# Fourteen unused products at the start of a vision-transformer kernel, while its embedding weights land

## The reference

```python
h = tok(x)                       # layernorm(768) -> @ W + bias -> layernorm(256) -> + positions, class tokens
h = h + attn0(layernorm(h))      # 16 heads, causal; weights quantised by the mean of |w|
h = h + tanh(layernorm(h) @ weight @ aux1 @ aux2 + bias)
h = h + attn1(layernorm(h))      # 16 heads, biases, head mask
h = h + moe(layernorm(h))        # top 1 of 16 experts, 256 -> 1024 -> 256, capacity 76
```

## Time and profile before

| | |
|---|---|
| median of 3 runs | 361.79 us (361.61 to 362.27) |
| profiled execution | 363.0 us |
| its span | 361.2 us |
| TensorE busy | 332.7 us (92% of the span) |
| VectorE, ScalarE, GpSimd busy | 193.6, 173.9, 170.2 us |
| mean granted clock of TensorE | 0.966 |

### The profile page before, as it was taken

How to read it: one execution, slowest core, us unless ns; L and a number is a source line. 1 busy time by engine, 2 the same in 40 slices (tenths; PEclk the granted TensorE clock), 3 DMA queues, 4 the chain that set the end, 5 groups by cost and what they waited for, 6 DMA issues and landing times.

```text
span 361.2 us, 8897 instructions
## 1 busy us (share of the span) xinstructions
PE 332.7 (92%) x3230; PEld 241.1 (67%) x3230; DVE 193.6 (54%) x520; ACT 173.9 (48%) x505; POOL 170.2 (47%) x289
## 2 busy tenths in 40 slices
PE   1975998999999999999999998979899999999993
PEld 1854887787888887878788876759356455454361
DVE  0376364576857648577686888681153252351350
ACT  1680685544566566666756655360253143342350
POOL 0255289765666757676977666643002102112012
PEclk9996799999999999999999999687999999999999
DMA  7999910114361724155523222412999999993500
GB/s 237 410 355 390 368 32 28 52 52 141 102 211 58 250 78 151 54 165 178 184 76 113 83 78 77 154 38 80 392 370 409 361 365 367 312 373 104 163 12 10
DMA packets 40835, 67.11 MB, mean 186 GB/s; under 512 B 4942, under 2 KB 31889, under 8 KB 39961
## 3 DMA queue, kind: packets, MB, share of 16 engines
q1 hardware_dynamic: 36696, 57.29, 45.8%
q10 hardware_dynamic: 2448, 7.03, 5.3%
q0 software_dynamic: 1648, 2.24, 1.8%
HBM read 54.14 MB, written 8.48 MB: 173 GB/s over the span
## 4 chain that ended last, share of the span: by engine, by line
PE 76%; DMA 7%; POOL 6%; SPq 3%; DVE 3%; issue 3%; ACT 0%; POOLq 0%; DVEq 0%
PE bank L1057 12%; PE bank L1024 12%; PE bank L921 8%; PE bank L969 7%; PE bank L950 5%; PE bank L983 5%; PE bank L932 5%; PE bank L958 5%; PE bank L1035 3%; PE bank L990 3%; DMA early<-in_ffn 3%; SPq L675 3%; DMA mid<-in_table 3%; PE bank L897 2%; PE bank L906 2%
## 5 line engine op out<-in xcount | busy, mean ns | idle before, releaser
L832 POOL DMA_INDIRECT out<-mid,idx x12 | 11.7, 976 | 97.6 <-DVE mid L1412 97.6
L791 POOL TENSOR_TENSOR mid<-mid,tab 128x608 f32<-128x608 f32 x32 | 39.3, 1235 | 15.2 <-PE bank L950 11.9
L1057 PE MATMUL bank<-early,mid 128*64 128x256 f32 (+1 forms) x448 | 43.7, 381 | 0.0
L1209 ACT ACTIVATE mid<-bank,cols 128x64 f32<-128x64 f32 (+1 forms) x128 | 25.8, 332 | 25.1 <-PE bank L1035 25.1
L1322 DVE TENSOR_REDUCE mx<-bank 102x16 f32<-102x608 f32 x32 | 25.0, 783 | 22.8 <-PE bank L950 22.6
L1024 PE MATMUL bank<-early,mid 128*64 128x512 f32 (+1 forms) x192 | 36.2, 596 | 0.7 <-ACT mid L1192 0.7
L1057 PEld LDWEIGHTS bank<-early,mid 128*64 128x64 f32 (+1 forms) x448 | 25.2, 123 | 15.8 <-issue 2.9
L921 PE MATMUL bank<-xnT,attn 128*128 128x256 f32 (+1 forms) x160 | 34.9, 371 | 0.0
L897 PE MATMUL bank<-early 128*128 128x256 f32 (+2 forms) x120 | 30.0, 406 | 2.8 <-DVE tokens L1301 2.8
L921 PEld LDWEIGHTS bank<-xnT,attn 128*128 128x128 f32 x160 | 29.1, 190 | 3.6 <-issue 0.4
L776 POOL TENSOR_TENSOR rs<-rs,mhalf 128x1 f32<-128x1 f32 (+2 forms) x50 | 28.7, 574 | 4.2
(11 more groups left out here) (142 smaller groups left out, 649.3 us busy)
## 6 DMA issues: line engine op xcount, KB each, us to landing
early<-in_w SPq DMA_DIRECT2D x52, 512.0 KB, 7.1
v3a<-vt SPq DMA_DIRECT2D x102, 40.0 KB
early<-vt SPq DMA_DIRECT2D x90, 40.0 KB
expert_in<-k_empty SPq DMA_DIRECT2D x1, 3084.0 KB, 22.4
early<-in_xt ACTq DMA_DIRECT2D x2, 1152.0 KB, 19.7
early<-in_xf SPq DMA_DIRECT2D x2, 1152.0 KB, 11.7
xnT<-in_w SPq DMA_DIRECT2D x4, 512.0 KB
tokens<-in_w SPq DMA_DIRECT2D x4, 512.0 KB
```

Source lines behind the costliest of these rows:

```text
L791: eng.tensor_tensor(km[:, n % 2], bc(kT[:, :, n * PCOLS:(n + 1) * PCOLS], 2, 4), bc(bc(quarterm[:, :], 2, PCOLS), 1, KC), ALU.mult).then_i ...
L1057: ins = mm(Yp[m % 2][a * width:(a + 1) * width, 0:DIM], hT[:, m % 2, c, a * width:(a + 1) * width], w2s[e % W2_SLOTS][:, c, :], start=c == ...
L1209: ins = eng.activation(hT[:, m % 2, c, a * width:(a + 1) * width], Tp[0][:, c * 128 + a * width:c * 128 + (a + 1) * width], ACT.Relu, bias ...
```

## The change

Ahead of TensorE's list of steps it now waits for `ones` and runs fourteen products of `ones` with itself, 128x128 by 128x128 in float32, into the two halves of `Sp` in turn. Nobody reads them. The lists of all engines stay as they are.

```diff
                     pe.wait_ge(g_free[b], m)
                 return G[b], g_full[b]
 
+            pe.wait_ge(consts, 1)
+            for n in range(14):
+                mm(Sp[:, n % 2, 0:128], ones[:, :], ones[:, :], start=True, stop=True)
             done = {}
             for kind, l, n in order("pe"):
                 done[kind] = done.get(kind, 0) + 1
```

## The result

The changed kernel takes 364.26 us (median of 14 runs, 362.98 to 367.52), the kernel before 362.22 us in the same series (14 runs, 359.77 to 366.63). The ratio is 1.0064 with a 95% interval of 1.0034 to 1.0094, which is 2.3 us. The forecast was 362.1 us and no measurable change; 0.4 us of the distance to it is the kernel before itself, which stood at 361.79 us when the forecast was made. The profiled execution took 363.97 us, its span is 362.2 us.

The account below looks back on a forecast made before the run. The start was taken as bound by the landing of `in_ffn`, which fB waits for. Products 0, faster cs 0 at the end, fetch +0.3 us on 361.79 gave 362.1 us, range 360.9 to 363.0.

Parts of the forecast that it names:

- part 1: TensorE's start: the fourteen products, 28 records from about 1.15 us, take 3.1 to 5.9 us, ending before the weights at 7.84.
- part 2: First product cs: with the clock raised, its start to that of bs takes 2.6 us instead of 5.01, gaining 2.4 us.
- Its condition: Ahead of cs: the raised clock stays up over 1 to 2 us of idling; otherwise the gain at cs is 0.
- part 3: From cs to fB: of 2.4 us won, 1.5 remain after qs and become wait for `in_ffn`; gain at the end 0.
- part 4: TensorE's code on q8: 56 more instructions move its first packet ahead of the landing of `in_ffn`, delaying fB by 0.3 us.
- bounds of 0 and 1.1 us: Delay of fB: 0 if the fetching engine is early or the fetch doesn't move, 1.1 us if the whole packet is added.
- a fixed place in the stream: First q8 packet: if tied to the 167th recorded instruction, it comes 56 instructions earlier, in tile 2, near 21 us.
- the fetch: Rival at the landing of `in_ffn`: the fetching engine is among the last, adding 0.8 to 1.1 us; chance 0.10.
- The step after it: From fB to the end: all engines start again from fB, so the fetch's +0.3 us there counts fully in the time.
- No wait of TensorE for the code itself: TensorE during the fetch: no wait for code expected, since before the change it works through that stretch without a pause.
- The bound of 0.2%: Whole time: "same" means within 0.2%, 0.72 us, about what a measurement can tell from no change; chance of same 0.70.

Follow-up runs that it names:

- e5: Kernel before plus ten unused small products (40 instructions) at TensorE's start: 362.61 us, ratio 1.0011 to the kernel before.
- e2: Kernel before plus three unused products of 512 columns (12 instructions) at TensorE's start: 362.12 us, ratio 1.0025 to the kernel before.
- e1: Kernel before plus 113 waits of TensorE on the semaphore of `ones` (56 instructions), no unused product: 363.65 us, ratio 1.0061.
- e3: Kernel before plus seven unused small products (28 instructions) at TensorE's start: 362.51 us, ratio 1.0014 to the kernel before.
- e4: Kernel before plus three unused small products (12 instructions) at TensorE's start: 361.62 us, ratio 0.9984 to the kernel before.
- e6: Kernel before with `in_ffn` issued ahead of the patches of tiles 4 to 6, no unused products: 360.3 us, ratio 0.9938.
- e7: Kernel before with `in_ffn` issued ahead of SyncE's wait for the position table, no unused products: 359.47 us, ratio 0.9924.
- e10: Kernel before plus 337 waits of TensorE on the semaphore of `ones` (168 instructions), no unused product: 367.49 us, ratio 1.0108.
- e11: Kernel before with e7's early `in_ffn` and e5's ten unused products together: 361.04 us, ratio 0.9974 to the kernel before.
- e8: e7 with the fourteen unused products added in front: 362.26 us, ratio 1.0004 to the kernel before.
- e9: Kernel before plus twelve unused small products (48 instructions) at TensorE's start: 364.05 us, ratio 1.0021 to the kernel before.
- e12: Kernel before plus fourteen unused products, seven at the start and seven right ahead of tile 3: 364.15 us, ratio 1.006.

## Why the prediction was wrong, point by point

**The cost of the products** (part 1) held: 28 records from 1.15 us in 5.26 us, done at 6.4 us, ahead of the weights.

**The gain at cs** (part 2) held: from its start to that of bs it is 9.37 - 6.71 = 2.66 us where 2.6 was put down. Its condition wasn't put to the test here. The idle stretch ahead of cs was 0.29 us and not 1 to 2, because the weights landed early. e5 has 1.35 us and still a fast cs. The advice of the Trainium skill (TensorE: Matmul & The Clock Gate, "Why this matters for your kernels") to warm TensorE up is borne out for this one product, and its warning on gaps as well: from 37.49 us on, fB runs at half speed again (3.78 us, as in the earlier trace rows, with a granted clock of 0.50 up to 42.65 us).

**Where the gain goes** (part 3) held closely. qs came at 19.23 us (19.1 put down) and tile 3 at 24.85 (24.7). The 1.3 us won there became part of the wait before fB. e2 and e5 show this by itself: cs fast, time unchanged within the interval. But not all of the 1.3 us is owed to the warm-up. Kernels whose cs was slow while their weights landed nearly as early (e1, e3, e4, e6 and e7) start tile 3 at 24.98 to 25.50 us. That leaves 0.1 to 0.7 us for the faster cs; the rest is the early landing, which is chance.

**The fetch** (part 4) is the step that failed. Its direction was right and its size was not: the term of the sum was +0.3 us. The prediction named the packet, its move ahead of the landing and the late engine, and then took 0.3 us out of bounds of 0 and 1.1 us. Measured: 2.8 us at fB, 2.0 to 2.3 us at the end. The upper bound was no bound. It took the duration of the packet (1.1 us) for the delay that it can cause; but the last part lands 2.1 us behind the third last, and the others are later too, 35.33 against 34.53 us. (In e2 to e5, where the packet stays late, the third last comes at 34.42 to 34.95, so a part of this last difference is chance.) That the packet moved as foreseen was partly luck. It was put near 21 us by a fixed place in the stream, the 167th recorded instruction; it came at 23.4 us, 180 recorded instructions in, and e3 and e5 show that there is no such fixed place. With ten products the same rule would have been wrong. Within the bounds I then chose the low part, on the ground that the engine serves other queues meanwhile. The case "the fetch" among the rivals had the right mechanism and sign, with a chance of 0.10 and a price of 0.8 to 1.1 us. The step after it held: e6 shows that what happens to fB reaches the end nearly whole, 2.3 us there and 2.2 at the end.

**The rest.** "No wait of TensorE for the code itself" held: the gap in which the packet falls is the one before tile 3, and VectorE ends it, 2.57 us long as before. The bound of 0.2% for what can be told apart was drawn from three runs within 0.66 us. Fourteen runs of the same kernel spread from 359.77 to 366.63 us, and twelve to fourteen runs gave intervals of about 0.3% to either side, so a loss of 0.3 us as predicted could not have been seen.

**What stays open.** Why a packet of 1.1 us delays a part by 2.1 us. The lateness isn't there at once: it is 1.5 us at 25.6 us, 2.7 at 30.4 and 2.1 from 35.6 us on. It is smaller for later packets: 1.7 to 2.1 us behind the third last for packets at 23.4 to 24.4 us, 1.3 in e10 at 29.9 (of which 0.6 was there before), 0.7 in e11 at 30.9 (0.8 before). In the time between lie small copies of the position table. In the changed kernel their last parts land at 32.1, 32.4, 32.6, 32.8 and 33.0 us, one by one, where before the last of them is at 30.3 us. That the small copies of the late engine, on the queue of SyncE, have to take turns with large packets of the other queue, and so lose more than the fetch itself takes, would fit; it is only argued, and was not tried. Open too is what decides when the packet starts. With nothing changed but the order of loads it moved from 38.7 us to 47.7 (e7), and with 40 instructions it came at 39.0 us in e5 and 30.9 in e11.

## What to carry to other kernels

When a step waits for a transfer, a faster step in front of it is worth nothing, but what delays the transfer is worth nearly its full price; the last of the sixteen parts decides. Instructions weren't free here even on an idle engine: their code comes by DMA too, and in this start, which keeps the DMA engines full, 56 extra instructions cost 2 us where 12 for the same warm-up (wide products instead of small ones) cost nothing that could be told from zero. The chain pointed to the better edit from the start: load what it waits for earlier, which gave 0.6% to 0.8%.

## What the runs showed of the hardware

A 16 KB packet of code takes 1.1 us on its DMA engine (1.10 us in before, 1.11 in after). With the packet at 23.4 to 24.4 us and the DMA engines full, the last part of later transfers came 1.7 to 2.1 us behind the third last, up to 14 us after the packet (after, e1, e8, e9, e12). The lateness wasn't made up while the queues were full: in the changed kernel the patches of tiles 4 to 6, `in_ffn` and the patches of tiles 7 to 9 land at 35.56, 37.44 and 40.19 us, each with its last part 2.1 us behind the third last. A wait of TensorE on a semaphore that has its value already costs about 0.05 us (337 of them 18 us in e10), or 0.11 us for each instruction that two waits make.
